# Window attention with a channel-correlation stage: squares and boxes of the second stage taken off TensorE, transposes with 113 columns

## The chip, the cores and the metric

One core of a Trainium2 chip. The metric is device time in microseconds for one execution, median of three runs.

## The reference

`x` is (32, 56, 56, 96), float32. Two residual blocks follow each other.

```python
x = x + window_attention(_gn(x))      # 7x7 windows, shifted by 3, 12 heads of 8, relative bias, masks
x = x + correlation(_gn(x))

def _gn(v):                           # 32 groups of 3 channels, over rows, columns and the group
    ...
    return (g - m) / jnp.sqrt(s + 1e-5)

def correlation(y):                   # box_sum pads with zeros
    s = box_sum(y, 2, 5)              # five neighbours along a row
    num = box_sum(s * s, 3, 20)       # twenty neighbours over channels
    d = box_sum(box_sum(y * y, 2, 5), 3, 20)
    norm = box_sum(ones(56), 0, 5)    # how many neighbours a place has
    return nan_to_num(num / (d * norm[None, None, :, None]), nan=1.0)
```

## The kernel before

All engines run one static list of work, written as a loop over slots `s` from -78 on. A function such as `units(s, at)` says which unit is due at slot `s`; every engine has its own order of calls inside a slot, and semaphores tie the engines together. The names are these:

- A step `j` is a pair of windows, 32 steps to an image, one step per slot (1024 in all). A unit `U` is a row of eight windows: four steps, so four slots. There are 8 units to an image.
- A group `G` is eight image rows of the second block, 7 groups to an image (224 in all); one group is due every four slots, and the eighth unit of an image has none. `X1` holds the result of the first block with channels on partitions.

What TensorE does in a slot: `scores(j)` (L448, into bank pair `pS`), `times_v(j)` (L475, into `pO`), then, by slot, `values` (L430), `normalise` (L558), `turn_x` (L381) or `turn_o` (L488), then `turn_scores` (L460, transposes of `T` for the softmax, into `pP`), `project_o` (L498), `turn_x1` (L607), `qk` (L388 to L390, q into `bankB`, k into `bankC`), `wide_squares` and `wide_y` (L572, L584), `deep_squares` and `deep_y` (L591, L598), and the small statistics products (L504, L510, L518, L521).

What VectorE does: `add_bias` (L775, frees `pS` for the next scores), `maximum` (L782), `low_k` (L794), `low_q` (L788), `invert_sums` and `divide_o` (L805, L812; they free `pO`), `add_residual` (L824), statistics (L830, L836 and single-column operations), and of the second block `scale_squares` (L913, writes `dent`), `scale_boxes` (L920, writes `numt`), `ratio` (L926, `numt` from `dent` and `numt`) and `result` (L933, writes `tok_out`).

ScalarE copies TensorE's results out of PSUM (`keep_v` L681, `keep_x` L662, `keep_o` L700, `high_qk` L670 and L672, `keep_y` L716 and L719, `keep_wide` L725 and L729), takes the exponentials (L691) and `invert` (L736, L739: reciprocal by Ln and Exp, the first with a bias operand from SBUF). GpSimd does `shift` (L1058, subtracts the maximum from `T`), `high_x` and `low_x` (L1030, L1036) and `wrap` (L1047). SP issues all DMAs.

The second block before: `normalise` multiplies X1 by a diagonal matrix with a bias row, `DG`, so that Y comes out with pixels on partitions; ScalarE stores Y and its square; `wide_y` and `wide_squares` sum along rows and bring channels back on partitions; ScalarE stores these, the box of Y squared; `deep_y` and `deep_squares` sum over channels. Denominator and numerator are in `bankB` and `bankC`, then `invert`, `scale_squares`, `scale_boxes`, `ratio`, `turn_x1` (into `bankC` again) and `result`.

Three banks are shared by order and by waits:

```python
def qk(U):
    ...
    project(bankB, 0, u, q_made)
    G = group_of(U - QK_AHEAD - 1)
    if G is not None:
        pe.wait_ge(out_made, G + 1)      # result has read bankC
    ...
    project(bankC, C, u, k_made)

def scores(j):
    ...
        pe.wait_ge(biased, j)            # add_bias has read pS
```

Of the kernel before, what the change touches and what calls it, by code (L numbers as in the profile page):

```python
# [15 lines left out]
L = WIN * WIN  # L16
# [15 lines left out]
TILES = 4  # L32
GROUPS = SIDE // (2 * TILES)
# [9 lines left out]
LOAD_AT, FILL_AT, STATS_AT, HIGH_AT, LOW_AT = -78, -50, -49, -28, -26  # L43
# [7 lines left out]
NORM2 = dict(aggr=38, mean=39, dev=40, var=40, root=41, scale=42, bias=42, fold=43)  # L51
# [7 lines left out]
K_COUNT = K_WIDE + ROWS2  # L59
K_N = K_COUNT + ROWS2  # L60


def shape_constants():
# [10 lines left out]
    for h in range(2):  # L74
        rows = slice(SIDE * h, SIDE * h + SIDE)
        k[rows, K_WIDE + SIDE * h:K_WIDE + SIDE * h + SIDE] = near
        k[rows, K_COUNT + SIDE * h:K_COUNT + SIDE * h + SIDE] = near * near.sum(0)[None, :]
# [28 lines left out]
def group_of(k):  # L106

    m, v = divmod(k - Y_AT // 4, UNITS)
    return GROUPS * m + v if 0 <= m < IMAGES and v < GROUPS else None


def groups(s, at):
    k = s - at
    if k % 4:
        return []
    g = group_of(k // 4 + Y_AT // 4)
    return [] if g is None else [g]
# [6 lines left out]
def build(nc, x, wT, bias_row, pT, pb_row, flipped, consts, out):  # L124
    ctx = ExitStack()
    with ctx:
# [16 lines left out]
        wide = K[0:ROWS2, K_WIDE:K_WIDE + ROWS2]  # L143
        wide_count = K[0:ROWS2, K_COUNT:K_COUNT + ROWS2]
# [5 lines left out]
        DG = sb("DG", [C + 1, C])  # L150
# [89 lines left out]
        PE_LINKS, ACT_LINKS, DVE_LINKS = 3, 2, (16, 12)  # L240
        y_made = signal("y_made")
        sq_kept = signal("sq_kept")
        y_kept = signal("y_kept")
        wsq_made = signal("wsq_made")
        wsq_kept = signal("wsq_kept")
        wy_made = signal("wy_made")
        wy2_kept = signal("wy2_kept")
# [118 lines left out]
        def _(pe):  # L366

            def turn_x(U):
# [3 lines left out]
                G = group_of(k)  # L372
                if G is not None:
                    pe.wait_ge(y_kept, G + 1)
                elif k >= 0:
# [76 lines left out]
            def turn_scores(j):  # L452
# [26 lines left out]
            def turn_o(U):  # L479
# [3 lines left out]
                elif group_of(U + 1) is not None:  # L483
                    pe.wait_ge(y_kept, group_of(U + 1) + 1)
                elif U + 1 < ALL_UNITS:
                    pe.wait_ge(v_kept, 2 * (U + 2))
                for p in range(PAIRS):
                    mm = pe.transpose(bankA[0:C, 128 * p:128 * p + 128], O[U % 2][:, p, :], ident)  # L488
# [24 lines left out]
            def norm_bias(m, which):  # L513

                pe.wait_ge(norm_dve[which], DVE_LINKS[which] * m + 10)
                wait_for_statistics_bank(m, which, "bias")
                if which:
                    pe.matmul(bankA[C:C + 1, 0:C], g[1][:, NB:NB + 1], ident[0:C, 0:C], start=True, stop=True  # L518
                              ).then_inc(norm_pe[1], 1)
                else:  # L520
                    pe.matmul(bankA[C:C + 1, 0:3 * C], g[0][:, NB:NB + 1], WT[0:C, :], start=True, stop=True  # L521
                              ).then_inc(norm_pe[0], 1)

            def wait_for_statistics_bank(m, which, link):

                s = STEPS * m + (NORM1, NORM2)[which][link]
                for U in units(s, V_AT):
                    pe.wait_ge(v_kept, 2 * U + 2)
                for G in groups(s, Y_AT):
                    pe.wait_ge(y_kept, G + 1)  # L530
# [5 lines left out]
            def wait_for_statistics(s):  # L536

                for which, at, reads in ((0, NORM1, (2, 5, 12)), (1, NORM2, (2, 5, 11))):
                    for link, read in zip(("mean", "var", "bias"), reads):
                        for m in images(s - 1, at[link]):  # L540
                            pe.wait_ge(norm_dve[which], DVE_LINKS[which] * m + read)

            def normalise(G):
                m, v = divmod(G, GROUPS)
                if v == 0:

                    pe.wait_ge(norm_dve[1], DVE_LINKS[1] * m + 12)
                    pe.wait_ge(wrapped, (UNITS + 1) * (m + 1))
                k = (STEPS * m + 4 * v + Y_AT) // 4
                if k < ALL_UNITS:  # L550
                    pe.wait_ge(v_kept, 2 * (k + 1))
                elif k - 2 < ALL_UNITS:
                    pe.wait_ge(o_kept, k - 1)
                else:
                    pe.wait_ge(y_kept, G)
# [6 lines left out]
            def wide_squares(G):  # L562
                k = STEPS * (G // GROUPS) // 4 + G % GROUPS + Y_AT // 4
                pe.wait_ge(sq_kept, G + 1)
# [542 lines left out]
```

## Time and profile before

| what | value |
|---|---|
| median of 3 runs | 3903.43 us (3903.14 to 3905.89) |
| profiled execution, its time | 3903.11 us |
| its span in the trace | 3901.3 us |
| TensorE matmuls busy | 3737.0 us, 96% |
| weight loads busy | 3244.5 us, 83% |
| VectorE busy | 3169.5 us, 81% |
| ScalarE busy | 2097.6 us, 54% |
| GpSimd busy | 1686.3 us, 43% |

The span runs from the first to the last instruction of the trace; the execution's own time is 1.8 us longer. Busy times of TensorE overlap from one instruction to the next, since matmuls are pipelined: how long a batch holds the engine is read from the start of one batch to the start of the next, not from its duration. A row of a timeline merges neighbouring instructions of the same line; in brackets it gives the time in which the engine stood idle before it and what ended that.

### The profile page before, as it was taken

How to read it: one execution, taken by the hardware profiler on the slowest of the kernel's cores; microseconds unless marked ns; L12 is line 12 of the kernel's file. 1: busy time of each engine (PE TensorE's matmuls, PEld its weight loads, DVE VectorE, ACT ScalarE, POOL GpSimd, SP SyncE). 2: the span in 40 equal slices, each digit the busy share in tenths (PEclk: the TensorE clock that was granted, in tenths of full speed). 3: DMA queues.
4: the chain of work that ended last, by engine and by line, in shares of the span. 5: the costliest groups of instructions: out<-in, count | busy, mean ns of one | idle time of the engine just before them, and what ended most of it. 6: DMA issues, size and time to landing. Idle time of an engine off the chain costs nothing.

```text
span 3901.3 us, 156374 instructions
## 1 busy us (share of the span) xinstructions
PE 3737.0 (96%) x65536; PEld 3244.5 (83%) x65536; DVE 3169.5 (81%) x5647; ACT 2097.6 (54%) x4033; POOL 1686.3 (43%) x1843
## 2 busy tenths in 40 slices
PE   5899999999999999999999999999999999999997
PEld 3788888888888888888888888888888888888887
DVE  5888888888888888888888888888888888888872
ACT  2455555555555555555555555555555555555553
POOL 4544444444444444444444444444444444444430
PEclk9999999999999999999999999999999999999996
DMA  3332232233233233233322322322322332332220
GB/s 81 78 78 68 73 82 69 73 77 74 70 78 77 68 74 79 69 75 77 74 71 74 79 71 73 81 67 73 82 70 71 77 76 69 77 78 58 66 53 20
DMA packets 385728, 280.81 MB, mean 72 GB/s; under 512 B 261927, under 2 KB 384904, under 8 KB 385032
## 3 DMA queue, kind: packets, MB, share of 16 engines
q1 hardware_dynamic: 385032, 270.81, 28.3%
q8 instruction: 525, 8.60, 1.0%
q14 instruction: 171, 1.40, 0.1%
HBM read 39.35 MB, written 38.54 MB: 20 GB/s over the span
## 4 chain that ended last, share of the span: by engine, by line
PE 76%; DVE 13%; issue 5%; SPq 4%; ACT 1%; DMA 1%; POOL 0%; DVEq 0%; ACTq 0%; POOLq 0%
PE pP L460 14%; PE pO L475 11%; PE pS L448 8%; PE pM L558 5%; PE pM L572 4%; PE pM L591 4%; PE pM L584 4%; PE pM L598 4%; PE pM L430 3%; PE pM L381 3%; PE pM L488 3%; PE pM L498 3%; PE pM L388 2%; DVE MX L782 2%; DVE T L775 2%
## 5 line engine op out<-in xcount | busy, mean ns | idle before, releaser
L1058 POOL TENSOR_TENSOR T<-T,MX 128x588 f32<-128x588 f32 x1024 | 1213.0, 1185 | 2114.9 <-DVE MX L782 2114.8
L775 DVE TENSOR_TENSOR T<-pS,table 128x588 f32<-128x588 f32 x1024 | 785.0, 767 | 328.5 <-PE pS L448 313.1
L460 PE MATMUL pP<-K,T 128*128 128x128 f32 x6144 | 870.5, 278 | 0.8 <-issue 0.5
L691 ACT ACTIVATE P<-pP 128x588 f32<-128x588 f32 x1024 | 677.7, 662 | 208.3 <-PE pP L460 202.1
L782 DVE TENSOR_REDUCE MX<-T 128x12 f32<-128x588 f32 x1024 | 768.2, 750 | 2.1
L475 PE MATMUL pO<-V,P 128*49 128x18 f32 x24576 | 716.8, 197 | 39.1 <-DVE O L812 39.0
L475 PEld LDWEIGHTS pO<-V,P 128*49 128x49 f32 x24576 | 696.1, 125 | 46.9 <-ACT P L691 41.4
L460 PEld LDWEIGHTS pP<-K,T 128*128 128x128 f32 x6144 | 674.7, 141 | 26.4 <-issue 0.7
L448 PE MATMUL pS<-KE,QS 128*64 128x196 bf16 (+1 forms) x8192 | 474.1, 234 | 13.0 <-DMA KE<-KS 11.4
L681 ACT ACTIVATE V<-pM 49x384 f32<-49x384 f32 x512 | 264.1, 516 | 376.2 <-PE pM L430 370.0
L448 PEld LDWEIGHTS pS<-KE,QS 128*64 128x64 bf16 x8192 | 290.2, 109 | 180.2 <-issue 94.2
L716 ACT ACTIVATE SQ<-pM 112x384 f32<-112x384 f32 x224 | 110.1, 491 | 457.4 <-PE pM L558 457.4
L788 DVE TENSOR_TENSOR qnl<-pM,qnh 96x392 bf16<-96x392 f32 x256 | 143.8, 562 | 203.3 <-ACT qnh L670 203.3
L662 ACT ACTIVATE X<-pM 96x392 f32<-96x392 f32 x256 | 134.9, 527 | 287.9 <-PE pM L381 272.2
L700 ACT ACTIVATE OT<-pM 96x392 f32<-96x392 f32 x256 | 126.5, 494 | 294.4 <-PE pM L488 294.4
L926 DVE SCALAR_TENSOR_TENSOR numt<-dent,numt 112x384 f32<-112x384 f32 x224 | 241.4, 1078 | 24.4 <-DVE numt L920 1.4
L1036 POOL TENSOR_TENSOR XL<-X,XH 96x392 bf16<-96x392 f32 x256 | 238.1, 930 | 0.6
L558 PE MATMUL pM<-DG,X 97*112 97x96 f32 x1792 | 233.0, 274 | 0.8 <-DVE DG L907 0.8
L430 PE MATMUL pM<-WH,XH 97*64 97x48 bf16 x4096 | 225.5, 190 | 1.1 <-DVE W L885 1.1
L430 PE MATMUL pM<-WH,XL 97*64 97x48 bf16 x4096 | 225.8, 190 | 0.5 <-issue 0.5
L430 PE MATMUL pM<-WL,XH 97*64 97x48 bf16 x4096 | 225.6, 190 | 0.0
L388 PE MATMUL pM<-XH,WH 97*96 97x392 bf16 x512 | 179.4, 350 | 43.6 <-DVE X L824 30.1
(95 smaller groups left out, 6787.8 us busy)
## 6 DMA issues: line engine op xcount, KB each, us to landing
KE<-KS SPq DMA_DIRECT2D x512, 147.0 KB, 2.9
KS<-knh SPq DMA_DIRECT2D x768, 49.0 KB, 2.0
QS<-qnh SPq DMA_DIRECT2D x768, 49.0 KB, 2.0
out<-tok_out SPq DMA_DIRECT2D x384, 84.0 KB
tok_in<-x SPq DMA_DIRECT2D x224, 84.0 KB
KS<-knl SPq DMA_DIRECT2D x384, 49.0 KB, 2.0
QS<-qnl SPq DMA_DIRECT2D x384, 49.0 KB, 2.0
tok_in<-x SPq DMA_DIRECT2D x224, 63.0 KB
```

What stands on the lines that cost most here:

```text
L388: pe.matmul(dst[0:C, 0:TOK], WH[:, col:col + C], XH[:, xs], start=True, stop=False)
L430: mm = pe.matmul(bankA[64 * h:64 * h + 64, col:col + C // 2], lhs, wv[:, :, h, :], start=(part == 0), stop=(part == 2))
L448: mm = pe.matmul(pS[64 * w:64 * w + 64, bank, col:col + (h1 - h0) * L], Q[:, gq, at:at + 64], E[:, h0:h1, at:at + L], start=True, stop=True)
L460: mm = pe.transpose(pP[:, c, 128 * at:128 * at + 128], T[j % 4][:, 2 * h:2 * h + 2, :], ident)
L475: mm = pe.matmul(pO[64 * w:64 * w + L, col:col + VC], P32[j % 3][:, 2 * h + w, :], V[U % 2][:, 2 * p + w, h, :, :], start=True, stop=True)
L558: mm = pe.matmul(bankA[0:ROWS2, C * t:C * t + C], X1[m % 2][:, at:at + ROWS2], DG[:, :], start=True, stop=True)
L681: act.activation(V[U % 2][ps, :, :, h, 0:D], bankA[ps, 0:PAIRS * C].rearrange("p (w a d) -> p w a d", w=UNITS, d=D), ACT.Copy).then_inc(v_ ...
L691: act.activation(P32[j % 3][:, :, :].rearrange("p (c a) q -> p c a q", c=2), src, ACT.Exp).then_inc(p_made, 1)
L775: dve.tensor_tensor(T[j % 4][:, :, 0:L].rearrange("p (b h) k -> p b h k", b=2), pS[:, :, 0:HALF].rearrange("p b (h k) -> p b h k", k=L), t ...
L782: dve.tensor_reduce(MX[j % 4][:, :], T[j % 4][:, :, 0:L], AX.X, ALU.max).then_inc(maxed, 1)
L926: dve.scalar_tensor_tensor(out=numt[:, :], in0=dent[:, :], scalar=-2.0, in1=numt[:, :], op0=ALU.add, op1=ALU.mult).then_inc(ratio_made, 1)
L1058: pool.tensor_tensor(t, t, MX[j % 4][:, :].unsqueeze(2).broadcast_to([128, HEADS, L]), ALU.subtract).then_inc(shifted, 1)
```

## The change

Along the code:

- The affine normalisation moves to ScalarE: `normalise` writes Y with channels on partitions, in rows of 60 with zeros at both ends, and `square` writes its square, both straight from `X1` with scale and bias from SBUF. `DG`, `fold_norm2`, the bias product of norm 2 and the ones row of `X1` go.
- The box of Y along a row becomes three additions on GpSimd (`pairs_of_y`, `fours_of_y`, `box`), each in another slot; `square_box` on ScalarE squares it.
- `deep_squares` sums the squares over channels first; `keep_squares` copies that to SBUF, and `wide_squares` is one product along the row, with the neighbour counts in its matrix. `wide_y` goes; `deep_y` stays.
- `turn_scores` and `turn_o` transpose 113 rows with a 113x113 permutation instead of 128 with the identity, and ScalarE reads 98 columns in a piece.
- Slots: `high_x` from -28 and `low_x` from -26 both to -27; the second block's stages are spread from 45 to 54 instead of 45 to 50. Groups are counted from slot 50 instead of 45, so the unit without a group falls four slots later at the stages of TensorE.

```diff
-LOAD_AT, FILL_AT, STATS_AT, HIGH_AT, LOW_AT = -78, -50, -49, -28, -26
+LOAD_AT, FILL_AT, STATS_AT, HIGH_AT, LOW_AT = -78, -50, -49, -27, -27
-Y_AT, WIDE_AT, DEEP_AT, RATIO_AT, OUT_AT, STORE_AT = 45, 46, 47, 48, 49, 50
+Y_AT, PAIR_AT, FOUR_AT, BOX_AT = 45, 46, 47, 48
+SQ_AT, DEEP_AT, WIDE_AT, RATIO_AT, OUT_AT, STORE_AT = 49, 50, 51, 52, 53, 54
...
-                    mm = pe.transpose(pP[:, c, 128 * at:128 * at + 128], T[j % 4][:, 2 * h:2 * h + 2, :], ident)
+                    mm = pe.transpose(pP[:, c, QN * at:QN * at + QN], T[j % 4][0:QN, 2 * h:2 * h + 2, :], pick)
...
-                    mm = pe.transpose(bankA[0:C, 128 * p:128 * p + 128], O[U % 2][:, p, :], ident)
+                    mm = pe.transpose(bankA[0:C, QN * p:QN * p + QN], O[U % 2][0:QN, p, :], pick)
...
-                for t in range(TILES):
-                    at = ROWS2 * (TILES * v + t)
-                    mm = pe.matmul(bankA[0:ROWS2, C * t:C * t + C], X1[m % 2][:, at:at + ROWS2], DG[:, :],
-                                   start=True, stop=True)
-                mm.then_inc(y_made, 1)
...
                 for t in range(TILES):
-                    mm = pe.matmul(bankB[0:C, ROWS2 * t:ROWS2 * t + ROWS2], SQ[:, t, :], wide_count,
+                    mm = pe.matmul(bankB[0:ROWS2, C * t:C * t + C], SQ[:, ROWS2 * t:ROWS2 * t + ROWS2], band,
                                    start=True, stop=True)
...
+            def wide_squares(G):
+                pe.wait_ge(csq_kept, G + 1)
+                pe.matmul(bankB[0:ROWS2, 0:TILES * C], wide_count, csq[:, :], start=True, stop=True
+                          ).then_inc(den_made, 1)
...
+            def normalise(G):
...
+                if G:
+                    act.wait_ge(ybox_step, 3 * G)
+                act.activation(Y[:, :, 2:2 + SIDE], x1, ACT.Identity,
+                               bias=g[1][:, NB:NB + 1], scale=g[1][:, RS:RS + 1]).then_inc(y_made, 1)
+
+            def square(G):
...
+                act.activation(SQ[:, :], X1[m % 2][:, GTOK * v:GTOK * v + GTOK], ACT.Square,
+                               bias=g[1][:, NB:NB + 1], scale=g[1][:, RS:RS + 1]).then_inc(sq_made, 1)
+
+            def square_box(G):
+                act.wait_ge(ybox_step, 3 * G + 3)
...
+            def pairs_of_y(G):
+                pool.wait_ge(y_made, G + 1)
+                pool.tensor_tensor(y2[:, :, 0:SIDE + 3], Y[:, :, 0:SIDE + 3], Y[:, :, 1:SIDE + 4], ALU.add
+                                   ).then_inc(ybox_step, 1)
+
+            def fours_of_y(G):
+                pool.wait_ge(ybox_step, 3 * G + 1)
+                pool.tensor_tensor(y4[:, :, :], y2[:, :, 0:SIDE], y2[:, :, 2:SIDE + 2], ALU.add
+                                   ).then_inc(ybox_step, 1)
+
+            def box(G):
+                pool.wait_ge(ybox_step, 3 * G + 2)
...
+                pool.tensor_tensor(ybox[:, :].rearrange("c (r w) -> c r w", w=SIDE), y4[:, :, :],
+                                   Y[:, :, 4:SIDE + 4], ALU.add).then_inc(ybox_step, 1)
...
             for s in range(FIRST_SLOT, END_SLOT + 1):
+                for G in groups(s, BOX_AT):
+                    box(G)
                 for j in steps(s + 1):
                     shift(j)
+                for G in groups(s, PAIR_AT):
+                    pairs_of_y(G)
+                for G in groups(s, FOUR_AT):
+                    fours_of_y(G)
                 for U in units(s, HIGH_AT):
                     high_x(U)
```

## Rows read from the trace of the kernel before

**Rows 1.** The page's chain that ended last, by engine.

```profile
PE 76%; DVE 13%; issue 5%; SPq 4%; ACT 1%; DMA 1%; POOL 0%; DVEq 0%; ACTq 0%; POOLq 0%
```

**Rows 2.** Timeline of TensorE's matmuls, one unit: start us, us, engine, line.

```profile
2003.69 0.46 PE L448 MATMUL pS<-KE,QS 128*64 128x196 bf16 x8
...
2006.09 0.82 PE L498 MATMUL pM<-OT,PT 97*96 97x392 f32 x2
2006.75 0.49 PE L607 MATMUL pM<-K,X 96*112 96x96 f32 x4
2007.17 0.46 PE L448 MATMUL pS<-KE,QS 128*64 128x196 bf16 x8
...
2008.09 1.03 PE L558 MATMUL pM<-DG,X 97*112 97x96 f32 x8
2008.95 0.82 PE L460 MATMUL pP<-K,T 128*128 128x128 f32 x6
...
2010.13 0.37 PE L388 MATMUL pM<-XH,WH 97*96 97x392 bf16 x1
...
2010.76 0.46 PE L448 MATMUL pS<-KE,QS 128*64 128x196 bf16 x8
...
2012.99 0.93 PE L572 MATMUL pM<-K,SQ 112*96 112x112 f32 x8
...
2014.62 0.46 PE L448 MATMUL pS<-KE,QS 128*64 128x196 bf16 x8
2014.90 0.70 PE L475 MATMUL pO<-V,P 128*49 128x18 f32 x24
...
2016.66 0.94 PE L591 MATMUL pM<-K,wsq 96*112 96x96 f32 x8
2017.44 0.95 PE L598 MATMUL pM<-K,wy 96*112 96x96 f32 x8
2018.32 0.46 PE L448 MATMUL pS<-KE,QS 128*64 128x196 bf16 x8
```

**Rows 3.** Timeline of VectorE, the same unit.

```profile
2004.21 0.77 DVE L775 TENSOR_TENSOR T<-pS,table 128x588 f32<-128x588 f32 x1 [1.32 <-PE pS L448]
...
2006.03 0.55 DVE L920 SCALAR_TENSOR_TENSOR numt<-pM,rd 112x384 f32<-112x384 f32 x1
2006.68 1.11 DVE L926 SCALAR_TENSOR_TENSOR numt<-dent,numt 112x384 f32<-112x384 f32 x1
```

**Rows 4.** Timeline of TensorE, around the statistics of both norms.

```profile
1246.34 0.46 PE L448 MATMUL pS<-KE,QS 128*64 128x196 bf16 x8
...
1257.05 0.37 PE L388 MATMUL pM<-XH,WH 97*96 97x392 bf16 x1 [0.37 <-DVE tok_out L933]
...
1261.66 0.73 PE L475 MATMUL pO<-V,P 128*49 128x18 f32 x24 [0.95 <-DVE O L812]
...
1283.79 0.46 PE L448 MATMUL pS<-KE,QS 128*64 128x196 bf16 x8
```

**Rows 5.** Timeline of VectorE, one slot C of that stretch.

```profile
1258.65 0.77 DVE L775 TENSOR_TENSOR T<-pS,table 128x588 f32<-128x588 f32 x1
...
1260.96 0.56 DVE L812 TENSOR_TENSOR O<-pO,rden 128x384 f32<-128x384 f32 x1
```

**Rows 6.** Groups of instructions by line and form: busy us, mean ns; idle before.

```profile
L1058 POOL TENSOR_TENSOR T<-T,MX 128x588 f32<-128x588 f32 x1024 | 1213.0, 1185 | 2114.9 <-DVE MX L782 2114.8
...
L1036 POOL TENSOR_TENSOR XL<-X,XH 96x392 bf16<-96x392 f32 x256 | 238.1, 930 | 0.6
...
L736 ACT ACTIVATE rd<-pM,tiny 112x384 f32<-112x384 f32 x224 | 130.2, 581 | 30.3 <-PE pM L591 6.1
```

**Rows 7.** Timeline of VectorE at the end, where GpSimd is idle.

```profile
3877.68 0.56 DVE L926 SCALAR_TENSOR_TENSOR numt<-dent,numt 112x384 f32<-112x384 f32 x1
...
3887.34 0.56 DVE L926 SCALAR_TENSOR_TENSOR numt<-dent,numt 112x384 f32<-112x384 f32 x1
```

**Rows 8.** Timeline of GpSimd, the unit of rows 2.

```profile
2006.19 1.18 POOL L1058 TENSOR_TENSOR T<-T,MX 128x588 f32<-128x588 f32 x1 [2.52 <-DVE MX L782]
```

More of the change, by code:

```diff
@@ L75, in shape_constants @@
         rows = slice(SIDE * h, SIDE * h + SIDE)
-        k[rows, K_WIDE + SIDE * h:K_WIDE + SIDE * h + SIDE] = near
-        k[rows, K_COUNT + SIDE * h:K_COUNT + SIDE * h + SIDE] = near * near.sum(0)[None, :]
+        k[rows, K_WIDE + SIDE * h:K_WIDE + SIDE * h + SIDE] = near * near.sum(0)[None, :]
+    order = np.concatenate([np.arange(L), 64 + np.arange(L), np.arange(L, 64)])
+    k[order, K_PICK + np.arange(QN)] = 1
     t = np.arange(L)
@@ L371, in turn_x @@
                 k = U - X_AHEAD
[L372 to L375, printed above, removed]
+                if k >= 0:
                     pe.wait_ge(v_kept, 2 * (k + 1))
@@ L536, in wait_for_statistics, with deep_squares @@
             def wait_for_statistics(s):
[L538 to L540 removed]
+                for which, at, links in ((0, NORM1, ("mean", "var", "bias")), (1, NORM2, ("mean", "var"))):
+                    for link, read in zip(links, (2, 5, 12)):
+                        for m in images(s - 1, at[link]) + images(s - 2, at[link]):
                             pe.wait_ge(norm_dve[which], DVE_LINKS[which] * m + read)
[L543 to L555, printed above, removed]
[L556 to L564 removed]
+            def deep_squares(G):
+                k = STEPS * (G // GROUPS) // 4 + G % GROUPS + DEEP_AT // 4
+                pe.wait_ge(sq_made, G + 1)
                 if k + QK_AHEAD < ALL_UNITS:
@@ L620, in _ @@
                     values(U)
-                for G in groups(s, Y_AT):
-                    normalise(G)
                 for U in units(s, FILL_AT):
@@ L634, in _ @@
                     qk(U)
+                for G in groups(s, DEEP_AT):
+                    deep_squares(G)
                 for G in groups(s, WIDE_AT):
                     wide_squares(G)
-                    wide_y(G)
-                for G in groups(s, DEEP_AT):
-                    deep_squares(G)
                     deep_y(G)
@@ L645, in _ @@
                         norm_variance(m, which)
-                    for m in images(s, at["bias"]):
-                        norm_bias(m, which)
+                for m in images(s, NORM1["bias"]):
+                    norm_bias(m)
         @block.scalar
@@ L745, in _ @@
                     keep_v(U)
+                for G in groups(s, SQ_AT):
+                    square(G)
                 for G in groups(s, Y_AT):
-                    keep_y(G)
+                    normalise(G)
                 for U in units(s, FILL_AT):
@@ L759, in _ @@
                     high_qk(U)
+                for G in groups(s, BOX_AT):
+                    square_box(G)
+                for G in groups(s, DEEP_AT):
+                    keep_squares(G)
                 for G in groups(s, WIDE_AT):
-                    keep_wide(G)
-                for G in groups(s, DEEP_AT):
                     invert(G)
@@ L982, in _ @@
                     fold_qk(m)
-                for m in images(s, NORM2["fold"]):
-                    fold_norm2(m)
                 for j in steps(s + 1):
```

142 lines of the change are left out of this document (62 added, 80 removed).

## The prediction

> **What bounds the kernel now.** I read the page's chain that ended last, then groups by line, then TensorE's, VectorE's and GpSimd's timelines over one unit. The chain [rows 1] is 76% TensorE, 13% VectorE. TensorE looks like the bound, so the tempting sum is TensorE time removed. The timelines say otherwise, and my forecast rests on them.
>
> A unit is four slots, each opened by a pair of windows' scores (L448). I call them A (values, transposes, projection, transpose of X1), B (normalise, transposes, q and k), C (load transposes, score transposes, the two wide products), D (O transposed, scores transposed, the two deep products). In [rows 2] A runs 2003.69 to 2007.17 = 3.48 us, B to 2010.76 = 3.59, C to 2014.62 = 3.86, D to 2018.32 = 3.70: 14.63 us. Two of these are held by VectorE although TensorE shows almost no idle time:
> - A: VectorE can begin the bias 0.52 us after the scores [rows 2, 3]; bias, dent, maximum and numt follow, and numt ends at 2006.03 + 0.55 = 2006.58. The transpose of X1 needs numt: it starts at 2006.75, which is also when the projection has been issued (2006.09 + 0.66). Two chains of equal length.
> - B: bias, residual, maximum, result, then the k projection into the bank that result has read. Image ends hold a slot B without normalise [rows 4]: there the k projections stand 0.37 us until VectorE's tok_out. In the regular slot, with normalise, k starts at 2010.13 = B + 2.96 [rows 2], and by VectorE's order (0.52, then bias, residual, maximum, result) that is when result ends: A's four operations took 2.89 from the scores, and B's four are of the same lengths. So again two equal chains.
>
> **The change, part by part.** Per group of eight rows (224 of them):
> - normalise on TensorE (8 passes) goes from B: 0.86 us of issue (2008.09 to 2008.95 [rows 2]). Cover by VectorE: all of it. B stays 3.59.
> - L572 and L584 (16 passes) go from C, and L591's product, now `deep_squares`, comes into C. L591's share is 2017.44 - 2016.66 = 0.78 [rows 2], so C is 3.86 - 0.78 = 3.08.
> - D loses L591 and gains `wide_squares`: one product streaming 384 columns. L498 streams 392 and takes 2006.75 - 2006.09 = 0.66 [rows 2]; D is 3.70 - 0.78 + 0.66 = 3.58. `deep_y` stays.
> - Score transposes: the streamed matrix shrinks from 128 to 113 columns, the loaded one stays 128 (T of two heads). A product that loads 112 and streams 96 columns (L591, 0.94 for eight) takes as long as one that loads 96 and streams 112 (L572, 0.93) [rows 2]: the larger of the two sets the pace, and it stays 128. I take 0, with 15/128 of about 0.66 for six (0.82 merged, less the overlap [rows 2]), 0.08 per slot, as the other end. O's four transposes load 96 and stream 128: 113 gives 15/128 of 4 x 0.11 = 0.05 in D, between 0 and that.
> - O's division. VectorE's C is bias, low half of k, maximum, reciprocal, division; [rows 5] has the bias at 1258.65 and the division's end at 1260.96 + 0.56, 2.87 after it. With the bias at C + 0.52 the division ends at C + 3.39 and the next unit's first product with V starts 0.14 later, as 1261.66 after 1261.52 [rows 4, 5]: C + 3.53. Today's C is longer than that, so nobody waits; at 3.08 the scores of D go through and the product waits 0.17 (it would be due 0.28 after them [rows 2]). From it to the end of D: 2014.90 to 2018.32 = 3.42, less 0.78, plus 0.66, less 0.05 = 3.25. C + D = 6.78 against 7.56.
> - Unit: 3.48 + 3.59 + 6.78 = 13.85, 0.78 less. TensorE alone would ask 14.63 - 0.86 - 0.78 - 0.78 + 0.66 - 0.05 = 12.82, 1.81 less: 1.03 us of it go into waits.
> - ScalarE: `keep_y`'s two and `keep_wide`'s two (PSUM) become square, normalise, square of the box, copy: four again. Square and normalise stand ahead of B's exponentials, but need nothing of that slot's TensorE; between the box square, done by about B + 0.5, and the transposes' end at B + 1.7 there is room for 1.2 us of them (my estimate from the slot's order). An activation of 384 columns with an operand from SBUF for its bias takes 0.58 [rows 6]; two take 1.16: 0 on the path, 0.2 at most.
> - GpSimd: three additions of 96 x 472, 448 and 448. Line through 588 elements at 1185 ns and 392 at 930 [rows 6]: 1.03, 1.00, 1.00; at 930/392 each they would be 1.12, 1.06, 1.06; at the former per element 0.90 to 0.95. In its queue `fours` (D) and `box` (A) stand between D's and A's shift. From the end of D's maximum to A's it has about 3.69, less a shift of 1.19 and its start of 0.07: 2.4 us for both, 2.0 wanted. `pairs` (C) and the moved high and low halves (B) end before the next maximum. 0 on the path in a normal unit.
> - The lock behind this: ratio (L926) takes 1.11 us in a unit and 0.56 where GpSimd is idle [rows 3, 7]; it starts at 2006.68, GpSimd's shift runs 2006.19 to 2007.37 [rows 8], and ratio ends 0.42 after it, at 2007.79. So it waits out the shift, and B's bias, due at 2007.17 + 0.52, has nothing to spare. The Trainium skill states this as a rule (SBUF — State Buffer, Who interferes with whom): a VectorE instruction with two SBUF inputs and a GpSimd one that reads SBUF exclude each other; the trace agrees. By that rule alone, without asking when each starts, three more additions would lengthen ratio; here they end before it.
> - Statistics. The light unit (no group) moves from the second norm's slots to the first's. Ten slots, 1246.34 to 1283.79 [rows 4], take 37.45 today. Walked with the same rules, the second norm's scale step meets high and low halves on GpSimd (this C's bias about 0.8 later than today), and this C and D now carry products; the first norm's slots lose theirs. Slot by slot after: D 3.7 + 0.17 for a statistics product = 3.87; A and B, held by VectorE with its extra small operations, as today, 7.47; C and D, with that late bias, the division ending at C + 4.63 and D's work of 3.25 behind it, 8.0; A 3.48 + 0.18 = 3.66; B, its bias at 1.1 instead of 0.5 behind ratio and three small operations, 4.3; C and D without products, but with VectorE's scale chain of six behind the division and `pairs`, 6.5; A 3.45. Sum 37.3, with no row for several of them: bounds 35.3 to 39.3. What goes with norm 2's fold is in this stretch.
> - The slot B after the stretch has no result to wait for: 3.59 becomes 3.03, 0.56 less.
>
> Per image: 22 slots outside the stretch hold six Cs and five Ds: 5 x 0.78 + 0.77 = 4.67, plus 0.56, plus 0.15 of the stretch = 5.4. Groups run beside attention from slot 45 to 1023, 30.5 images: 165 us. The first 45 slots have no group: 0. Tail: seven groups without attention, one per 9.66 us (two ratios [rows 7]), of five serial products; three go, one comes. I take 7 us, so 18 less (0 to 25). Sum 183. The profiled execution's own time was 3903.11, 0.3 under the runs' median: 3903.1 - 183 = 3720.
>
> **Rivals.**
> 1. TensorE was the bound and stays it: 1.81 x 224 = 405, and 18 in the tail, give 3480; with the transposes' 0.08 x 4 x 256 = 82, 3400. For it: busy in every slice, chain 76%. Against: both waits of [rows 4] (0.37 and 0.95), which occur exactly where its work is missing. 0.07.
> 2. Partial: the D wait or the stretch comes out better and transposes follow the streamed columns. Without the wait 0.16 x 190 = 30 more, transposes in C and D about 18, stretch 2 x 30.5 = 61: 3611 at best. 0.2. The Trainium skill (TensorE: Matmul & The Clock Gate, LDWEIGHTS) says weight loading goes by columns, not rows; the two rows of equal length above agree, and by it the transposes gain nothing.
> 3. Slower than before: GpSimd becomes the bound in A. If each addition costs c, the shift is late by 2c - 2.4, ratio waits it out, and B's bias with it. At 1.6 us each the 0.78 is used up; at 2.0 the unit is 15.45, and the run about 3903 + 0.82 x 190 = 4060. For it: additions whose rows are 59 of 60 elements, one operand shifted by one, are in no row. Against: the line above gives 1.0. 0.05. The Trainium skill (GPSIMD Engine Reference, Performance versus the Vector engine) has 4497 ns for 2048 elements; scaled that is an estimate of 1.0, the same side.
> 4. Milder: shift late by 0.3, or the stretch 2 longer: 3740 to 3810. 0.13.
>
> The forecast holds 0.55. Range: 3600 to 3800 leaves out the first, the third and part of the fourth; its own range is 3680 to 3750. A difference under 0.2% (8 us) can't be told from none. Faster 0.93, same 0.02, slower 0.05.
>
> **What would show it.** Right: A and B still about 3.5 and 3.6 apart in the scores, with k held for tok_out in B; C near 3.1; first V product of D held for O by about 0.2; six transposes as long as before; additions near 1.0 us; VectorE's busy share up to about 82%. Wrong if B's scores are under 3.2 apart, if GpSimd's shift starts after waiting for `box` rather than the maximum, or if ScalarE's square and normalise hold back qn.

## The result, and the profile after

The changed kernel takes 3941.31 us, the median of 8 runs (3908.65 to 3960.39), beside 3904.61 us (3903.14 to 3906.93) for the kernel before on the same chips: ratio 1.0089, interval 1.0056 to 1.0123. It is 0.9% slower; 3720 was forecast, and even 3800 was outside. The profiled execution was the fastest of the eight, 3908.65 us, so what its trace explains is 189 us of the miss.

The changed kernel's page: busy time, TensorE's granted clock in 40 slices (9 is 90% or more of 2.4 GHz), and the chain that ended last, which was 76% TensorE before [rows 1].

```profile
PE 3497.9 (90%) x60544; PEld 2833.1 (73%) x60544; DVE 3214.0 (82%) x5583; ACT 2200.3 (56%) x4033; POOL 2339.7 (60%) x2514
...
PEclk9999999889999999899989999998999999899996
...
PE 44%; DVE 29%; issue 17%; SPq 6%; ACT 2%; DMA 2%; POOL 0%; DVEq 0%; POOLq 0%
```

TensorE lost 6 points of its share, and 1.00 no longer holds throughout: the mean granted clock is 0.946, before 0.992. As there are two levels, the time at 1.2 GHz is twice the missing share of the span: 2 x 0.054 x 3907 = 422 us. Summed from windows of 4 us over the trace it is 421 us, before 66. Of these 74 and 63 lie in the tail, where no attention runs. I call the rest, 347 us and 3 us, the low time.

TensorE's timeline over one regular unit of the changed kernel, the counterpart of [rows 2]: A, B, C, D begin at 1445.13, 1448.55, 1452.20 and 1455.22.

```profile
1445.13 0.46 PE L450 MATMUL pS<-KE,QS 128*64 128x196 bf16 x8
...
1448.55 0.46 PE L450 MATMUL pS<-KE,QS 128*64 128x196 bf16 x8
...
1450.53 0.34 PE L390 MATMUL pM<-XH,WH 97*96 97x392 bf16 x1 [0.27 <-DVE X L803]
...
1451.58 0.37 PE L390 MATMUL pM<-XH,WH 97*96 97x392 bf16 x1 [0.38 <-DVE tok_out L907]
...
1452.20 0.46 PE L450 MATMUL pS<-KE,QS 128*64 128x196 bf16 x8
...
1455.22 0.46 PE L450 MATMUL pS<-KE,QS 128*64 128x196 bf16 x8
1455.74 0.73 PE L477 MATMUL pO<-V,P 128*49 128x18 f32 x24
...
1458.92 0.46 PE L450 MATMUL pS<-KE,QS 128*64 128x196 bf16 x8
```

3.42 + 3.65 + 3.02 + 3.70 = 13.79 us, where 13.85 was forecast. q waits for VectorE's residual, k for its result, and the product with V comes 0.52 after the scores of D, not 0.28. So the regular unit is as predicted. The miss lies elsewhere, in three places of each image and in the clock.

**Slot 8, an A slot with the second norm's deviation.** VectorE, then GpSimd, then TensorE.

```profile
1385.51 0.67 DVE L831 TENSOR_TENSOR g<-mv,g 96x1 f32<-96x1 f32 x1
1386.21 1.17 DVE L833 SCALAR_TENSOR_TENSOR g<-g,mv 96x1 f32<-96x1 f32 x1
1387.42 0.77 DVE L754 TENSOR_TENSOR T<-pS,table 128x588 f32<-128x588 f32 x1
1388.11 0.55 DVE L887 SCALAR_TENSOR_TENSOR dent<-pM,rd 112x384 f32<-112x384 f32 x1
```

```profile
1385.23 0.93 POOL L1017 TENSOR_TENSOR y<-y 96x448 f32<-96x448 f32 x1
1386.24 1.13 POOL L1024 TENSOR_TENSOR ybox<-y,Y 96x448 f32<-96x448 f32 x1
```

```profile
1388.80 0.87 PE L500 MATMUL pM<-OT,PT 97*96 97x392 f32 x2 [1.09 <-DVE dent L887]
```

Two operations on a single column take 0.67 and 1.17 us (0.15 and 0.21 in the kernel before, below): each has two SBUF inputs, and each ends when one of GpSimd's additions does (1386.16 and 1387.37). Everything behind them is late, and the projection waits 1.09 us for `dent`.

**Slot 16, the last of the ten-slot stretch, an A slot without a group.** It takes 4.38 us (1417.09 to 1421.47) where the forecast had 3.45. TensorE waits for a row of the folded weights:

```profile
1419.20 0.21 PE L432 MATMUL pM<-WH,XH 97*64 97x48 bf16 x2 [1.12 <-DVE W L867]
```

**Slot 30 and the unit after it.** The low part of V's folded weights (L881) meets the first addition, 0.94 us long; the slot's bias moves back, so the shift, and with it the two other additions.

```profile
1230.71 0.94 DVE L881 TENSOR_TENSOR WL<-W,WH 97x96 bf16<-97x96 f32 x1
1231.68 0.77 DVE L754 TENSOR_TENSOR T<-pS,table 128x588 f32<-128x588 f32 x1
...
1236.63 1.89 DVE L900 SCALAR_TENSOR_TENSOR numt<-dent,numt 112x384 f32<-112x384 f32 x1
1238.44 0.76 DVE L754 TENSOR_TENSOR T<-pS,table 128x588 f32<-128x588 f32 x1
```

```profile
1230.57 0.97 POOL L1012 TENSOR_TENSOR y<-Y 96x472 f32<-96x472 f32 x1
...
1234.82 0.93 POOL L1017 TENSOR_TENSOR y<-y 96x448 f32<-96x448 f32 x1
1235.82 1.14 POOL L1024 TENSOR_TENSOR ybox<-y,Y 96x448 f32<-96x448 f32 x1
1236.92 1.19 POOL L1047 TENSOR_TENSOR T<-T,MX 128x588 f32<-128x588 f32 x1
```

```profile
1239.82 0.34 PE L390 MATMUL pM<-XH,WH 97*96 97x392 bf16 x1 [1.05 <-DVE X L803]
```

The ratio waits out the last addition and the late shift, 1.89 us instead of 1.11, and q is held 1.05 us.

**The clock.** Stretches of this trace: busy us of PE, PEld, DVE, ACT and POOL with counts, granted clock, DMA share, GB/s.

```profile
1226.00:1240.00 14.00, 12.61 (x237) 10.50 (x238) 13.07 (x21) 8.86 (x16) 9.34 (x10) 1.00 0.21 53
1240.00:1252.00 12.00, 11.62 (x104) 9.60 (x103) 6.59 (x12) 3.98 (x8) 6.54 (x7) 0.57 0.51 122
...
1270.00:1286.00 16.00, 15.82 (x147) 13.07 (x148) 11.55 (x24) 5.65 (x12) 6.10 (x6) 0.57 0.43 103
```

Right behind q's wait the granted clock goes to 0.57, 1.2 GHz for most of 12 us, and again from 1270, behind a wait of 1.11 us for `dent`. TensorE is "busy" there, more than before the fall, but gets through 104 matmuls in 12 us (the same stretch at full clock, in e15 below, has 214): a full row of busy tenths hides it.

**The sum.** Intervals of the ratio over an image without a long fall are 28.56, 13.79 three times, 14.57, 15.56 and 15.88: 115.9 us. The forecast was 118.1 - 5.4 = 112.7. The ten-slot stretch (1381.43 to 1421.47) takes 40.04 us, forecast 37.3: 2.7 more. Of these 2.0 are in slots 8 and 9 (9.44 instead of 7.47), 0.9 in slot 16, and the other seven slots are, term by term, within 0.1 of the forecast. The B slot behind slot 30 takes 4.43 instead of 3.65: 0.8 more. The unit gives 0.3 back. That is 3.2 x 30.5 = 98 us. From the ninth image on every third has two long falls and takes 123.1 us, and the mean of 27 is 119.0: another 3.1 x 30.5 = 95. Together 193, for a miss of 189. The seven other executions were slower at a lower mean clock each, from 3926 us at 0.940 to 3960 us at 0.932: the falls vary from run to run, and at the median they cost some 33 us more.

### The profile page after: what moved, and what is told of

Its sections match the earlier page's. It is cut to its first block, busy times and chain, and to the rows that moved or that the text cites. A ratio compares the mean times of both kernels' runs of the same rounds, so it can differ in the third digit from the quotient of the medians.

```text
span 3906.9 us, 147002 instructions
## 1 busy us (share of the span) xinstructions
PE 3497.9 (90%) x60544; PEld 2833.1 (73%) x60544; DVE 3214.0 (82%) x5583; ACT 2200.3 (56%) x4033; POOL 2339.7 (60%) x2514
## 4 chain that ended last, share of the span: by engine, by line
PE 44%; DVE 29%; issue 17%; SPq 6%; ACT 2%; DMA 2%; POOL 0%; DVEq 0%; POOLq 0%
DVE MX L761 9%; PE pP L462 8%; PE pO L477 7%; PE pS L450 6%; DVE T L754 6%; PE pM L549 4%; PE pM L566 4%; PE pM L555 4%; SPq L313 3%; PE pM L490 3%; DVE numt L894 3%; PE pM L383 3%; DVE tok_out L907 2%; PE pM L390 2%; SPq L321 2%
## 5 line engine op out<-in xcount | busy, mean ns | idle before, releaser
L462 PE MATMUL pP<-K,T 113*128 113x113 f32 x6144 | 850.5, 277 | 0.6 <-ACT P L656 0.3
L477 PE MATMUL pO<-V,P 128*49 128x18 f32 x24576 | 750.4, 200 | 87.9 <-DVE O L791 77.4
L477 PEld LDWEIGHTS pO<-V,P 128*49 128x49 f32 x24576 | 724.5, 130 | 123.5 <-issue 84.6
L462 PEld LDWEIGHTS pP<-K,T 113*128 113x128 f32 x6144 | 649.4, 147 | 33.4 <-POOL T L1047 0.6
L900 DVE SCALAR_TENSOR_TENSOR numt<-dent,numt 112x384 f32<-112x384 f32 x224 | 264.2, 1179 | 24.4 <-DVE numt L894 1.4
L390 PEld LDWEIGHTS pM<-XH,WH 97*96 97x96 bf16 x512 | 65.8, 129 | 285.8 <-DVE tok_out L907 141.9
L566 PEld LDWEIGHTS pM<-K,ybox 96*112 96x112 f32 x1792 | 220.5, 184 | 71.6 <-issue 9.5
L1024 POOL TENSOR_TENSOR ybox<-y,Y 96x448 f32<-96x448 f32 x224 | 254.4, 1136 | 17.6
L500 PE MATMUL pM<-OT,PT 97*96 97x392 f32 x512 | 214.4, 500 | 33.9 <-DVE dent L887 33.9
L1012 POOL TENSOR_TENSOR y<-Y 96x472 f32<-96x472 f32 x224 | 217.0, 969 | 39.1 <-ACT Y L684 39.1
```

Source lines behind the costliest of these rows:

```text
L390: pe.matmul(dst[0:C, 0:TOK], WH[:, col:col + C], XH[:, xs], start=True, stop=False)
L462: mm = pe.transpose(pP[:, c, QN * at:QN * at + QN], T[j % 4][0:QN, 2 * h:2 * h + 2, :], pick)
L477: mm = pe.matmul(pO[64 * w:64 * w + L, col:col + VC], P32[j % 3][:, 2 * h + w, :], V[U % 2][:, 2 * p + w, h, :, :], start=True, stop=True)
L566: mm = pe.matmul(bankC[0:ROWS2, C * t:C * t + C], ybox2[:, ROWS2 * t:ROWS2 * t + ROWS2], band, start=True, stop=True)
L900: dve.scalar_tensor_tensor(out=numt[:, :], in0=dent[:, :], scalar=-2.0, in1=numt[:, :], op0=ALU.add, op1=ALU.mult).then_inc(ratio_made, 1)
L1024: pool.tensor_tensor(ybox[:, :].rearrange("c (r w) -> c r w", w=SIDE), y4[:, :, :], Y[:, :, 4:SIDE + 4], ALU.add).then_inc(ybox_step, 1)
```

## The experiments

Each is compared with the kernel before, run on the same chip. "Low time" is without the tail. Clock and low time are those of the one profiled execution; for e5 and e6 that was 15 and 19 us slower than the median.

| kernel | us | ratio (interval) | clock | low time, us |
|---|---|---|---|---|
| changed kernel | 3941 | 1.0089 (1.0056 to 1.0123) | 0.946 | 347 |
| e1 fillers on TensorE | 3847 | 0.9851 (0.9836 to 0.9866) | 0.981 | 75 |
| e2 additions on an eighth | 3731 | 0.9559 (0.9544 to 0.9574) | 0.986 | 33 |
| e3 before + 113 transposes | 3871 | 0.9914 (0.9898 to 0.9931) | 0.987 | 17 |
| e4 no two-input small operations | 3729 | 0.9550 (0.9533 to 0.9568) | 0.975 | 116 |
| e5 only the statistics of e4 | 3781 | 0.9620 (0.9593 to 0.9648) | 0.962 | 214 |
| e6 VectorE's order | 3732 | 0.9558 (0.9522 to 0.9594) | 0.928 | 474 |
| e7 both, e4 and e6 | 3471 | 0.8890 (0.8877 to 0.8904) | 0.974 | 109 |
| e8 before + order | 3880 | 0.9936 (0.9921 to 0.9951) | 0.985 | 51 |
| e9 before + 2 delays | 4014 | 1.0279 (1.0264 to 1.0295) | 0.986 | 51 |
| e10 e6 + fillers | 3774 | 0.9659 (0.9643 to 0.9675) | 0.949 | 313 |
| e11 e7 + fillers | 3558 | 0.9110 (0.9097 to 0.9124) | 0.991 | 0 |
| e12 e7 with 128 transposes | 3519 | 0.9012 (0.8998 to 0.9026) | 0.986 | 27 |
| e13 before + many delays | 4229 | 1.0826 (1.0808 to 1.0844) | 0.981 | 89 |
| e14b e7 + 2 delays | 3580 | 0.9175 (0.9153 to 0.9197) | 0.975 | 109 |
| e15 changed, 128 transposes | 3830 | 0.9805 (0.9790 to 0.9819) | 0.989 | 20 |
| e16 e13 + 113 transposes | 4234 | 1.0847 (1.0829 to 1.0865) | 0.966 | 215 |

**Whose waits.** e2 cuts the additions to one of their eight rows (the box of Y is wrong elsewhere):

```diff
...
-pool.tensor_tensor(y4[:, :, :], y2[:, :, 0:SIDE], y2[:, :, 2:SIDE + 2], ALU.add
+pool.tensor_tensor(y4[:, 0:1, :], y2[:, 0:1, 0:SIDE], y2[:, 0:1, 2:SIDE + 2], ALU.add
...
```

> The changed kernel with GpSimd's three additions on one of the eight image rows instead of all, so the box of Y is missing in seven of eight rows. Theory 1: the two idle spots of TensorE per image (slots 1 and 8) come from VectorE operations with two SBUF inputs that wait for an addition; without them ratio never takes 1.89, images take 112 to 114 us, the clock stays at 0.98 or more and the time is 3700 to 3760 us. Rival (the additions are harmless and VectorE's own order sets the images): over 3850 us.

e4 leaves the additions alone and takes the second SBUF input from VectorE's small operations, a column as scalar operand or the mean straight from PSUM; the subtractions of the fold go to GpSimd, a cast to ScalarE:

```diff
-dve.tensor_tensor(gw[:, DEV:DEV + 1], mw[:, 0:1], gw[:, MEAN:MEAN + 1], ALU.subtract)
+dve.tensor_tensor(gw[:, DEV:DEV + 1], mw[:, 0:1], bankA[0:C, 0:1], ALU.subtract)
...
-dve.tensor_tensor(col(SQR), col(R0), col(R0), ALU.mult)
+dve.tensor_scalar(col(SQR), col(R0), col(R0), None, ALU.mult)
...
-dve.tensor_tensor(WL[:, qk], W32[:, qk], WH[:, qk], ALU.subtract)
+pool.tensor_tensor(WL[:, cols], W32[:, cols], WH[:, cols], ALU.subtract)
```

> The changed kernel with the small statistics operations of VectorE rewritten so that none has two tensor inputs in SBUF (tensor_scalar with scalars from SBUF, the mean from PSUM), and the weight folding's subtractions on GpSimd, its cast for v on ScalarE. All additions stay. Theory 1: the idle spots of slots 1 and 8 shrink below 0.6 us, the 1.89 us ratio goes, images take 112 to 114 us and the clock stays at 0.98 or more: 3700 to 3760 us. Rival (the additions delay the chain through GpSimd's queue as such, not through the lock): the gaps stay, 3850 us or more.

3731 and 3729: with the additions in full but nothing of VectorE's to meet in these two places, all is regained that an eighth of the additions regains. The additions as such cost nothing that shows; the meetings do. e5 is the half of e4 that touches the small statistics operations and leaves the fold.

> The changed kernel, with only the small statistics operations of a norm made single-input (a scalar operand from a column in place of a second SBUF tensor; the mean read from PSUM); the two subtractions that fold the scale into low parts stay two-input. Theory: of the two places per image where VectorE waits for GpSimd's additions, the deviation steps go (0.67 and 1.17 us to about 0.15), with the 1.09 us that the output product waited; the stretch at fold_v with its 1.89 us ratio stays, and with it one of the two falls of the granted clock. Image about 115 in good ones; 3850 (3800 to 3900). Rival 'both places are one cause' : about 3730 as with all locks removed. Rival 'the small operations cost nothing': 3920 to 3960.

3781 is below the 3800 to 3900 of the theory: both places count, the first for more than I had put on it. Slot 8 in VectorE's timeline of e5:

```profile
1106.27 0.15 DVE L831 TENSOR_TENSOR g<-mv,pM 96x1 f32<-96x1 f32 x1
1106.46 0.27 DVE L833 TENSOR_SCALAR g<-g,mv 96x1 f32<-96x1 f32 x1
```

0.67 and 1.17 us have become 0.15 and 0.27. Its undisturbed image takes 112.6 us and e4's 112.0. That the first is the forecast's 112.7 is in part luck: its ten-slot stretch takes 36.7 us, not 37.3, and the 0.8 us of slot 30, which the forecast did not have, are still in it. Low time of 214 us stays.

**What holds the regular unit.** The forecast had A and B held by VectorE. e6 reorders VectorE's calls within a slot and nothing else:

```diff
+for U in units(s, X1_AT):    add_residual(U)      # was behind add_bias and dent
 for j in steps(s + 1):       add_bias(j)
...
-for j in steps(s + 1):       maximum(j)           # was ahead of numt and ratio
 for G in groups(s, RATIO_AT): scale_boxes(G); ratio(G)
 for G in groups(s, OUT_AT):  result(G)
 for U in units(s, O_AT):     invert_sums(U); divide_o(U)
+for j in steps(s + 1):       maximum(j)
+for U in units(s, QK_AT):    low_q(U)             # was ahead of invert_sums
```

(The lines are drawn together, and the comments are mine.)

> The changed kernel with VectorE's order in a slot changed and nothing else: residual before the bias additions, then numerator, ratio, result, reciprocal and division of O, and the maximum and q's low part last. Theory (the regular unit is held by what VectorE's queue puts ahead of the ratio and of q's low part): B's slot falls from 3.65 to 3.0 or less, the unit from 13.79 to 12.5 to 12.9, near TensorE's own sum; the places with the lock and the clock falls remain, so 3650 to 3800. Rival (the unit is held by GpSimd's chain of shift, additions and ratio, whatever the order): unit 13.6 to 13.9, time within 30 of 3941. Rival (maximum later delays the exponentials): unit above 14, 4000 or more.

> Both edits: no two-input VectorE statistics or folding operation beside GpSimd's additions, and the changed VectorE order. Theory: unit 12.5 to 12.9, image 103 to 106, time 3420 to 3560, with the granted clock near the 0.99 of the kernel before. Rival (the order gives nothing): 3730 as with the first edit alone. Rival (GpSimd's chain bounds the unit at 13.8): 3700 to 3740.

> Control: the kernel before with the same change of VectorE's order. There TensorE sets the regular unit (no idle spot from VectorE of its size), so the theory expects little: 3880 to 3905. If it gained 100 or more, the order would be a gain of its own and no property of the changed kernel.

The theory held in all three, e8 at the edge of its range (3880) and e7 with a clock of 0.974 where 0.99 was expected. The unit falls from 13.79 to 12.51 us, and e7 is 11.1% faster than the kernel before. In the kernel before the same order gives 0.6%: there TensorE's own chain is equally long. TensorE's timeline of e7, one unit:

```profile
1180.22 0.46 PE L453 MATMUL pS<-KE,QS 128*64 128x196 bf16 x8
...
1182.86 0.46 PE L453 MATMUL pS<-KE,QS 128*64 128x196 bf16 x8
...
1184.38 0.80 PE L465 MATMUL pP<-K,T 113*128 113x113 f32 x6
1185.02 0.94 PE L552 MATMUL pM<-K,SQ 96*112 96x96 f32 x8
1185.88 0.46 PE L453 MATMUL pS<-KE,QS 128*64 128x196 bf16 x8
...
1189.32 0.46 PE L453 MATMUL pS<-KE,QS 128*64 128x196 bf16 x8
...
1192.73 0.46 PE L453 MATMUL pS<-KE,QS 128*64 128x196 bf16 x8
```

B has gone from 3.65 to 2.64 us, D from 3.70 to 3.44, and no wait of TensorE stands in it.

**The transposes where TensorE is the bound.** e3 puts only the 113x113 transposes into the kernel before; e12 takes them back out of e7.

> The kernel before with the 113-column transposes alone. As in the trace of the changed kernel, six score transposes take 0.63 instead of 0.71 us. Theory 1 (slots A and B are held by VectorE): only slots C and D get shorter, 0.08 + 0.12 a unit, 3904 - 50 = 3850 us, A stays 3.48 and B 3.59. Rival (TensorE-bound): 0.08 x 1024 + 0.05 x 256 = 95 us, 3810 us. Prediction on record (no gain in the score transposes): 3890 us.

> Both edits, but with the transposes of scores and of O as they were before (128x128 against a full identity); the rest as in the 3471 us kernel. There TensorE sets the unit (12.51 us), so what the 113x113 form gains shows in full. Theory: 0.08 us per slot for the scores and about 0.1 in D: unit 12.9, time 3560 to 3590. Rival (the prediction's nothing for the score transposes): 3470 to 3490.

e3 came out midway between its theory and the prediction's nothing: its unit is 14.43 us against 14.63, since VectorE holds A and B. e12's unit is 12.86 against 12.51, as its theory had it, but the time rose by 47 us only, under the 90 expected: fewer units of an image than I had counted are regular, and the low time fell from 109 to 27. TensorE's timeline of e12, slot C:

```profile
1088.47 0.87 PE L465 MATMUL pP<-K,T 128*128 128x128 f32 x6
1089.18 0.94 PE L552 MATMUL pM<-K,SQ 96*112 96x96 f32 x8
```

Six transposes take 0.71 us there and 0.64 in e7 (1184.38 to 1185.02).

**The clock.** First fillers: one to six small products of no use, into free columns of `pO`, where TensorE waits: ahead of q and of k in every B slot, of the projection in slot 8 and of the values in slot 16.

```diff
+def fill(n):
+    for _ in range(n):
+        pe.matmul(pO[0:C, 432:512], K[0:C, 0:C], K[0:C, 0:80], start=True, stop=True)
```

> The changed kernel with filler products on TensorE (float32, 80 columns, into the unused columns of the bank of O) where it stands idle: one before the q projections and two before the k projections of every slot B, 4 more in slot 1 and 3 more in slot 9 of an image, 6 each before the projection of slot 8 and the values of slot 16. They change no result. Theory 1 (TensorE's clock falls to its lower level after slots in which the engine stood idle for a microsecond, and that ate the gain): the granted clock stays near 1.00 as before the change, images take about 116 us instead of 119 on average, and the time is 3800 to 3840 us. Rival (the waits themselves cost the gain, the clock little): the time stays within 20 us of 3940, or rises, since nothing waits for less.

> The order edit (3732 us, low clock 539 us in all) with the filler products of the first experiment in TensorE's idle spots. Theory: low clock falls to 300 us or less and the time to 3600 to 3690. Rival (the time is set by VectorE's waits and the clock costs nothing): within 20 of 3732.

> Both edits (3471 us, low clock 181 us of which 72 in the tail) with the filler products. Theory: at most the 109 us of low clock before the tail are there to be won, half of it in time, and the fillers cost TensorE about 0.5 us per unit where it is the bound (128 us in all): 3480 to 3600, a loss. Rival: 3400 to 3460.

e1: products that compute nothing take low time from 347 to 75 us and make the kernel 94 us faster, a little short of the theory. In e10 low time falls from 474 to 313 us, but the kernel is slower (3774 after 3732): the products cost more than the clock returned, so neither theory held. In e11 no low time was left outside the tail, and the kernel was 86 us slower for it, as expected.

My theory was that a wait of about 1 us lets the clock fall. e9 makes such waits in the kernel before; e13 adds a shorter delay in every B slot.

```diff
+if s > 0 and s % STEPS in (8, 30):
+    dve.wait_ge(spared, ...)
+    dve.memset(spare[:, :], 0.0).then_inc(spared, 1)      # 128 x 2300
```

> The kernel before, whose granted clock falls for 66 us in all, with one addition: at two slots per image (8 and 30) VectorE first clears a spare tile, about 2.0 us of pure delay; nothing computed changes. Theory (an idle spot of TensorE of about 1 us inside its steady work is followed by a fall of the granted clock to 1.2 GHz): besides 1 to 1.5 us of direct wait per spot (65 to 95 us in all) the total of low clock grows to 250 us or more, and the time to 4030 to 4150. Rival (the falls come from something else in the changed kernel, such as GpSimd's additions): low clock stays at 60 to 120 us, time 3960 to 4000.

> The kernel before with the two clears of 2.0 us per image of the earlier run (4014 us, low clock 72 us in all, no more than without them) and a clear of about 0.95 us in every B slot, which loosens TensorE throughout. Nothing computed changes. Theory (falls of the granted clock follow stretches in which TensorE is idle by some 1 us in each unit as well as in one larger spot): low clock rises to 250 us or more, time 4250 or more. Rival (falls belong to what the changed kernel computes, GpSimd's additions above all): low clock stays at 60 to 120 us, time 4080 to 4250.

The 72 us of low clock which the second text gives for e9 were counted up to 3960 us; with the whole tail it is 118, of which 51 before the tail, where the kernel before has 3. For e13 it is 162 in all, not the 68 that the text for e16 gives, and 89 before the tail. TensorE's timeline of e9 behind one delay:

```profile
1250.91 0.98 PE L586 MATMUL pM<-K,Y 112*96 112x112 f32 x8 [1.27 <-DVE knl L796]
```

A wait of 1.27 us, longer than the 1.05 behind which the changed kernel's clock fell, and here it stayed at 1.00. It did so behind 18 of 28 such waits; behind the other 10 it fell for under 4 us. The changed kernel's own waits say the same, counted over its trace: behind q's wait of 1.05 us the clock falls in 10 images of 28, behind the 1.1 us for `dent` in nearly all, and behind its waits of 1.40 us (the product with V, 18 times) never. e9 is 109 us slower than the kernel before, the delays and 48 us more of low time together, and so lands between its two forecasts. With e13 loose throughout, low time is 89 us. That refuted the theory that a wait by itself does it. It left the work itself. e15 is the changed kernel with the old transposes, e16 is e13 with the new ones, e14b is e7 with two delays, each of two clears of 128 x 1040 (e14, with e9's 128 x 2300, does not fit into SBUF and has no time).

```diff
-mm = pe.transpose(pP[:, c, QN * at:QN * at + QN], T[j % 4][0:QN, 2 * h:2 * h + 2, :], pick)
+mm = pe.transpose(pP[:, c, 128 * at:128 * at + 128], T[j % 4][:, 2 * h:2 * h + 2, :], ident)
```

> The changed kernel with the transposes of scores and of O in their old 128x128 form, all else as changed, the waits for GpSimd's additions too. Theory (shorter transposes with the same idle spots are part of what lets the clock fall): low clock, 421 us in the changed kernel, under 250 us, and since VectorE holds the unit anyway, the time is 3850 to 3930, no slower than the 3941 us of the full change. Rival (the transposes have nothing to do with the clock): low clock 380 or more, time 3930 to 3990.

> The kernel before with the 113x113 transposes, and VectorE's clears of e13 (about 2.0 us at slots 8 and 30, 0.95 us in every B slot). Without the shorter transposes the low clock was 68 us in all and the time 4229 us. Theory (shorter transposes plus a loose TensorE bring the falls): low clock 200 us or more and 4230 or more. Rival (neither, the additions or the sums of squares do it): low clock under 120, time 4190 to 4230.

> Both edits (3471 us, low clock 181 us) with two pairs of clears of a spare tile on VectorE per image, about 1.9 us at slot 8 and at slot 30 each. The kernel before answered such a delay with no fall of the clock. Theory (the changed kernel's TensorE work is what is prone to falls, idle spots only tip it): low clock 300 us or more, 3620 or more. Rival (a full TensorE carries such a spot here too): direct delay of 65 to 110 us, low clock 180 to 250: 3540 to 3600.

e15 takes 3830 us. The shorter transposes make the changed kernel 111 us slower. The waits are still there, but two of them are shorter, 0.79 instead of 1.05 us for q and 0.91 instead of 1.09 for `dent`: the longer transposes fill a part of them. Here TensorE's timeline of e15 and then its stretches (columns as above):

```profile
1209.59 0.34 PE L390 MATMUL pM<-XH,WH 97*96 97x392 bf16 x1 [0.79 <-DVE X L803]
...
1235.57 0.87 PE L500 MATMUL pM<-OT,PT 97*96 97x392 f32 x2 [0.91 <-DVE dent L887]
1245.76 0.73 PE L477 MATMUL pO<-V,P 128*49 128x18 f32 x24 [1.27 <-DVE O L791]
```

```profile
1196.00:1210.00 14.00, 13.15 (x238) 11.01 (x238) 12.95 (x21) 8.76 (x16) 9.13 (x10) 1.00 0.22 55
1210.00:1222.00 12.00, 11.62 (x214) 9.61 (x213) 9.64 (x17) 6.96 (x13) 9.27 (x10) 1.00 0.51 121
...
1240.00:1256.00 16.00, 13.53 (x240) 11.15 (x240) 13.88 (x29) 8.02 (x15) 6.69 (x8) 1.00 0.36 84
```

The second stretch, the one behind q's wait, holds 214 matmuls in 12 us; the changed kernel's had 104. The image takes 116.0 us, and nearly all do. e16 against e13 shows it from the other side, the same stretch of each; first e13, then e16:

```profile
1224.00:1240.00 16.00, 13.07 (x273) 10.07 (x273) 15.03 (x31) 5.97 (x12) 5.79 (x6) 1.00 0.44 109
```

```profile
1224.00:1240.00 16.00, 14.41 (x192) 11.35 (x193) 12.75 (x28) 5.78 (x12) 6.08 (x7) 0.68 0.37 90
```

Low time goes from 89 to 215 us with nothing changed but the transposes (and the waits that they leave, some 0.1 us longer for q), and the 5 us by which e16 is slower than e13 stand where e3 gained 34. In e14b, where TensorE is full but for the two delays, it is 109, the same as without them. So neither part does it alone (e3: new transposes, full TensorE, 17 us; e15: old ones, waits, 20): the low time comes with both. Whether it is the shorter streams or the longer waits behind them that the clock answers, no run separates: none gives the changed kernel its old transposes and waits of the full 1.05 and 1.1 us. Nothing of the box of Y or of the squares is needed for it, though the changed kernel's 347 us are not reached by e16.

## Why the prediction was wrong

- **Right:** that TensorE's 76% of the chain was not the bound in A and B. The unit is 13.79 (13.85), C 3.02 (3.08), D 3.70 with the product held 0.24 (3.70 and 0.17), k held for `tok_out` 0.38, VectorE 82% busy. e6 shows the hold itself. Rival 1, TensorE as the bound, is out for this kernel. That e7 reaches 3471, near this rival's 3480, takes two further edits and does not speak for it.
- **Right:** the additions and the tail. GpSimd's groups by form: 3.04 us for three, forecast 3.03, and 6.87 us per group at the end (VectorE's ratios), forecast 7.

```profile
L1024 POOL TENSOR_TENSOR ybox<-y,Y 96x448 f32<-96x448 f32 x224 | 254.4, 1136 | 17.6
...
L1012 POOL TENSOR_TENSOR y<-Y 96x472 f32<-96x472 f32 x224 | 217.0, 969 | 39.1 <-ACT Y L684 39.1
L1017 POOL TENSOR_TENSOR y<-y 96x448 f32<-96x448 f32 x224 | 209.1, 934 | 0.7
```

```profile
3888.39 0.56 DVE L900 SCALAR_TENSOR_TENSOR numt<-dent,numt 112x384 f32<-112x384 f32 x1
3895.25 0.56 DVE L900 SCALAR_TENSOR_TENSOR numt<-dent,numt 112x384 f32<-112x384 f32 x1
```

- **Mis-sized, without effect:** ScalarE's normalise and square take 0.75 us each, not 0.58; GpSimd's first addition waits for the former (39 us in all), TensorE for neither beside attention.
- **Mis-sized, the stretch.** "Sum 37.3 ... bounds 35.3 to 39.3": 40.04, above its upper bound. The walk priced the additions against the ratio alone, and in A "with its extra small operations, as today". These have two SBUF inputs in slot 8, and today nothing of GpSimd's meets them there. Slots 8 and 9 took 9.44 us for the 7.47 of the sum. The other mis-sized term of the stretch is its last slot, "A 3.45": 4.38, with the wait for the folded weights in it; e5 takes it to 4.04, and what holds the rest was not tested. VectorE's timeline of the kernel before shows both cases of the same operation, free in slot 8 and, five slots later, against a shift:

```profile
1250.49 0.15 DVE L852 TENSOR_TENSOR g<-mv,g 96x1 f32<-96x1 f32 x1
1250.68 0.21 DVE L854 SCALAR_TENSOR_TENSOR g<-g,mv 96x1 f32<-96x1 f32 x1
...
1267.17 1.17 DVE L852 TENSOR_TENSOR g<-mv,g 96x1 f32<-96x1 f32 x1
```

The mechanism was on the page of the prediction; I asked it of one VectorE instruction instead of all that have two inputs. The Trainium skill's rule on two SBUF inputs (SBUF — State Buffer, Who interferes with whom) names no lower limit of size. The trace agrees, with 0.15 us turned into 0.67 and 0.21 into 1.17 for one column.
- **Missing, slot 30.** "22 slots outside the stretch" were taken as regular. The fold of V's weights was in none of the terms; it meets `pairs_of_y` and costs 0.8 us per image.
- **Missing, the clock.** The sum has no term for the granted clock; 0.992 before was taken as given. It costs 95 us in the profiled execution. The median is 33 us above that execution, and the runs' clocks, 0.946 in this one and 0.932 to 0.940 in the others, say that this is clock too.
- **The transposes:** "I take 0" was wrong by size where TensorE is the bound, 0.35 us per unit (e12), near the other end given, 0.08 per slot. In the changed kernel itself they gain little on the path, since VectorE sets it (unit 13.91 us in e15, 13.79 here), and the kernel is 111 us slower with them, which the clock accounts for. The step that failed is "the larger of the two sets the pace, and it stays 128": 0.71 against 0.64 us per six shows that the streamed columns count too, and the two rows of equal length in [rows 2], 112 loaded and 96 streamed or the reverse, could not show it. The Trainium skill (TensorE: Matmul & The Clock Gate, LDWEIGHTS) says that a weight load goes by its columns. The trace agrees as far as that goes, with 128 columns loaded in 141 ns before and 147 after; that the product behind the load gains nothing does not follow from it.
- **Rival 3** had the right sign and engine but another mechanism: the shift is late only in slot 30's train, not in every unit.

What stays open: why transposes of 113 columns and waits for VectorE together let the clock fall, and whether by the columns or by the longer waits. That each has a share was shown by a run; what the clock responds to was not.

## What to carry to other kernels

Before adding GpSimd work, list every VectorE instruction with two SBUF inputs, however small, and walk each one against the new instructions; moving one input to a scalar operand or to PSUM removed these waits at no cost. When an engine sheds work, look at who sets the unit then: here reordering VectorE's queue was worth more than the change (3941 to 3732, and 3471 with both edits). And read the granted clock beside the busy share in the profile after: a saving on an engine that waits anyway can be paid for in clock.

## What the runs showed of the hardware

- The granted clock fell to 1.2 GHz right behind waits of 1.05 us (in 10 images of 28) and of 1.09 to 1.11 us (in nearly all) in the changed kernel. It stayed at 2.4 behind waits of 1.40 us in the same kernel, of 1.27 us in e15 and behind 18 of 28 waits of 1.27 us in e9. The length of one wait doesn't tell.
- Useless products can pay: e1 is 94 us faster than the changed kernel. Where TensorE is the bound they don't (e11, 86 us slower than e7).
- Six fp32 transposes that load 128 columns take 0.71 us streaming 128 and 0.64 streaming 113: the streamed columns count here.
- A VectorE operation on one column waits for a whole GpSimd addition (0.15 to 0.67 us), as one on 384 columns waits for the shift (0.56 to 1.11, and 1.89 behind an addition and the shift).
